# A Mamba layer stack on one core: scaled identities for the scan's inputs, wide activations, and a planned order for every engine

## The reference

```python
h1 = relu(bn(einsum('bchw,oc->bohw', x, nin_w)))
xs = concatenate([v, flip(v, 2), flip(v, 1), flip(v, (1, 2))])     # four directions
u, z = split(einsum('blc,ic->bli', xs, in_proj_w))                  # 256 channels each
uc = silu(causal_conv4(u) + conv_b)
dtr, B, C = split(uc @ x_proj_w.T)                                  # 8, 16, 16 columns
dt = softplus(dtr @ dt_proj_w.T + dt_proj_b)
h_t = exp(dt_t * A) * h_{t-1} + (dt_t * u_t) * B_t                  # 16 states per channel
y_t = sum_n h_t[n] * C_t[n]
out = ((y + uc * D) * silu(z)) @ out_proj_w.T
```

## Time and profile before

| | us |
|---|---|
| Median of three runs | 13713.5 |
| The profiled execution, its own time | 13695.55 |
| Its span, first to last instruction | 13693.8 |
| POOL busy | 13045.4 (95%) |
| DVE busy | 12477.9 (91%) |
| ACT busy | 11898.3 (87%) |
| PE busy | 11889.6 (87%) |
| Mean granted clock of TensorE | 0.946 of full speed |

### The profile page before, as it was taken

The page is one execution under the profiler, slowest core; times in us unless marked ns, Lnnn a source line. Parts: engine busy times, 40 slices in busy tenths (PEclk is TensorE's granted clock), DMA queues, the critical chain, the costliest instruction groups (busy, mean ns, idle before and its releaser), DMA issues.

```text
span 13693.8 us, 182039 instructions
## 1 busy us (share of the span) xinstructions
PE 11889.6 (87%) x67228; PEld 8271.3 (60%) x67228; DVE 12477.9 (91%) x8406; ACT 11898.3 (87%) x18047; POOL 13045.4 (95%) x3978
## 2 busy tenths in 40 slices
PE   7888888888888888888888888888888888888886
PEld 4566666666666666566666566665666666666654
DVE  7899999999999999999999999999999999999985
ACT  6888888888888888888888888888888888888884
POOL 7999999999999999999999999999999999999995
PEclk8999999999999999999999999999999999999997
DMA  5566566656566666566665665655666656666552
GB/s 191 224 226 228 228 224 230 235 224 229 221 235 232 228 228 226 226 230 233 226 230 221 233 231 226 230 226 226 234 230 225 230 223 230 233 227 228 226 213 115
DMA packets 544698, 3067.83 MB, mean 224 GB/s; under 512 B 60378, under 2 KB 60474, under 8 KB 281538
## 3 DMA queue, kind: packets, MB, share of 16 engines
q1 hardware_dynamic: 543810, 3056.18, 59.1%
HBM read 2990.40 MB, written 48.76 MB: 222 GB/s over the span
## 4 chain that ended last, share of the span: by engine, by line
POOL 33%; PE 22%; issue 16%; ACT 13%; DVE 9%; DMA 4%; POOLq 0%; DVEq 0%; SPq 0%; ACTq 0%
POOL ring L983 24%; PE work L1481 10%; POOL ring L966 8%; PE y_acc L1496 7%; DVE ring L1469 6%; ACT ring L1160 3%; ACT L1000 3%; DMA cb_rows_scratch<-stack 2%; PE y_acc L1481 2%; DVE slot L1455 2%; PE slot L1496 1%; DMA b_rows<-cb_rows_scratch 1%; PE slot L1481 1%; ACT slot L1160 1%; ACT z_t L1069 1%
## 5 line engine op out<-in xcount | busy, mean ns | idle before, releaser
L983 POOL TENSOR_TENSOR ring<-ring,c_rows 128x2048 f32<-128x2048 f32 x2048 | 9297.0, 4548 | 392.6 <-DVE ring L1469 375.4
L1469 DVE TENSOR_TENSOR_SCAN ring<-ring,slot 128x1024 f32<-128x1024 f32 x2560 | 5817.8, 2280 | 218.7 <-PE slot L1496 82.3
L1496 PE MATMUL y_acc<-wk,ring 128*128 128x128 f32 x32768 | 4513.7, 284 | 671.7 <-POOL ring L983 656.5
L1496 PEld LDWEIGHTS y_acc<-wk,ring 128*128 128x128 f32 x32768 | 3984.0, 147 | 1506.1 <-POOL ring L983 850.8
L1469 DVE TENSOR_TENSOR_SCAN ring<-slot,ring 128x1024 f32<-128x1024 f32 x1536 | 3495.0, 2276 | 370.4 <-POOL ring L966 266.4
L966 POOL TENSOR_TENSOR ring<-du,b_rows 128x1024 f32<-128x1024 f32 x1536 | 3634.2, 2369 | 64.7 <-DMA b_rows<-cb_rows_scratch 53.3
L1160 ACT ACTIVATE ring<-dt,a_neg 128x1024 f32<-128x1024 f32 x2560 | 2846.2, 1139 | 19.6 <-PE y_acc L1496 9.8
L1000 ACT ACT_TABLE_LOAD x1883 | 2415.9, 1283 | 33.7
L1455 DVE TENSOR_TENSOR slot<-du,slot 128x1024 f32<-128x1024 f32 x1856 | 2246.1, 1210 | 73.5 <-PE slot L1481 71.4
L1481 PE MATMUL work<-h_new,fused 128*128 128x512 f32 x4096 | 1936.5, 603 | 8.6 <-DVE padded L1334 3.1
L1160 ACT ACTIVATE slot<-dt,a_neg 128x1024 f32<-128x1024 f32 x1536 | 1707.1, 1113 | 240.6 <-DVE ring L1469 230.6
(11 more groups left out here) (178 smaller groups left out, 9934.9 us busy)
## 6 DMA issues: line engine op xcount, KB each, us to landing
c_rows<-cb_rows_scratch SPq DMA_DIRECT2D x2048, 1024.0 KB, 4.7
b_rows<-cb_rows_scratch SPq DMA_DIRECT2D x1536, 512.0 KB, 5.6
x_next<-in_x SPq DMA_DIRECT2D x32, 512.0 KB, 5.6
x_new_scratch<-x_next SPq DMA_DIRECT2D x32, 512.0 KB, 7.8
h_old<-h_new SPq DMA_DIRECT2D x32, 512.0 KB, 7.9
x_old<-x_new_scratch SPq DMA_DIRECT2D x32, 512.0 KB, 10.1
out<-x_old SPq DMA_DIRECT2D x32, 512.0 KB, 7.9
cb_rows_scratch<-stack SPq DMA_DIRECT2D x128, 116.0 KB
```

Of the source, the lines that this page charges most:

```text
L983: pool.tensor_tensor(pair, pair, c_rows[:, k % CB_BUFS, :, :], ALU.mult).then_inc(prod_ready, 1)
L1469: dve.tensor_tensor_scan(slot, a, b, 0.0, MUL, ADD).then_inc(scan_done, 1)
L1496: ins = pe.matmul(chunk(out_t, j), chunk(x, j), kc("ident"), is_transpose=True, start=start and j % (BANK // P) == 0, stop=stop, skip_grou ...
```

## The change

- **Kinds.** 46 D, 46 P and 36 Z units.
- **Z units.** ACT now scales the 128x128 identity, not du_t, by the B of the tokens (`zmul`, kc("ident") in place of du_t). The tile depends on direction and state alone, so both channel halves use it: 18 tiles per image serve 36 units. Six tiles are kept (`Z_BUFS`). PE multiplies du_t by the tile, an ordinary FP32 matmul (`turn_z`), where it was a transpose.
- **Wide steps.** silu, softplus, dt_copy and dt_u take both PSUM banks in one instruction of 1024 columns.
- **Passes.** The order of halves within directions alternates, so that the second pass of a direction and the first of the next have the same half and add up in `y_acc`: takes go from 7 to 5, and half of the adds of `yz` into `y_acc` fall away.
- **Group norm sums** of layers 1 to 3 come from the copies that write x (`accum_out`) in place of separate passes.
- **Free order.** Units' inputs and products, spreads and sums, b and scan are streams of their own in the planner, with new costs and shifts; an input may come as early as its ring slot is free. The planner does not look at the row loads, apart from those after a new direction's rows.
- **Buffers.** `CB_BUFS`, `B_BUFS` 4 to 3, three u_conv tiles for four. `store_rows` moves from SP to ACT, right behind the step that fills the rows.
- Decays of P units are in PSUM as before.

```diff
-KINDS = ('DPDPZDDDDPZPDPDZ', 'DPDZDPDZDPZPDPDP', 'DDDDDPZPDPPPZDDP', 'DPDPDPZZPPZZDPDP',
+KINDS = ('DDPPZPZPPDZDZZPP', 'DPPDZDZPPDZDZZPP', 'DDPDZPZDDPZDPPZZ', 'DDDDZPZPDPZPPPZZ',
 ...
-CB_BUFS = 4
-B_BUFS = 4
-Z_BUFS = 2
+CB_BUFS = 3
+B_BUFS = 3
+Z_BUFS = 6
+Z_STEPS = 4
 ...
-SUM_LATER = 4
 SHIFTS = [
-    (-413, 123, -1143, -1629, -1503, -1060, -1344, -1469, -1469, -2434, -2294, -1545, -1418, -1624, -1701, -489,
+    (-41, -1, 17, -17, 247, 112, -42, 84, -281, 71, 39, 41, -29, 121, -143, -315, -355, -257, -182, -36, -141, -301,
 ...
+def unit_flows(kind):
+    of = lambda *kinds: [u for u in range(UNITS) if kind_of(u) in kinds]
+    turned = of("D", "Z")[kind != "first":] + [UNITS] * (kind != "last")
+    return {"D": [[("b", u) for u in of("D")], [("scan", u) for u in range(UNITS)]],
+            "G": [[("input", u) for u in of("P")], [("prod", u) for u in range(1, UNITS, 2)]],
+            "P": [[("zturn" if kind_of(u) == "Z" else "spread", u) for u in turned], [("sum", u) for u in range(UNITS)]],
+            "A": [[("decay", u) for u in range(UNITS)]]}
 ...
-            def store_rows(d, base, rows_done):
-                sp.wait_ge(*done(base, rows_done))
-                sp.dma_start(cb_dram[d].rearrange("(n t) -> n t", t=TOK), cb_rows).then_inc(cb_out, 16)
+            def store_rows(d, rows_done):
+                act.wait_ge(*rows_done)
+                act.dma_start(cb_dram[d].rearrange("(n t) -> n t", t=TOK), cb_rows).then_inc(cb_out, 16)
 ...
-                if k >= CB_BUFS or s > 0:
-                    sp.wait_ge(prod_ready, s * PAIRS + k - CB_BUFS + 1)
+                if loads >= CB_BUFS:
+                    sp.wait_ge(prod_ready, loads - CB_BUFS + 1)
 ...
-                    for j in range(4 * i, 4 * i + 4):
-                        ins = act.activation(z_t[:, turned % Z_BUFS, j * P:(j + 1) * P], du_t[:, j * P:(j + 1) * P], ACT.Copy,
-                                             scale=b_t[:, d % 2, j * NST + n:j * NST + n + 1])
+                    for j in range(CH // Z_STEPS * i, CH // Z_STEPS * (i + 1)):
+                        ins = act.activation(z_t[:, tile_of(u), j * P:(j + 1) * P], kc("ident"), ACT.Copy,
+                                             scale=b_turned(d, s)[:, j * NST + n:j * NST + n + 1])
 ...
-                    ins = act.activation(w, w, ACT.Softplus, bias=kc("dt_b", name[2], name[2] + 1))
+                    ins = act.activation(both_banks(w), both_banks(w), ACT.Softplus, bias=kc("dt_b", name[2], name[2] + 1))
 ...
-                    turn(operand[u % 2], z_t[:, (s * N_Z + number("Z", u)) % Z_BUFS, :], True, True).then_inc(z_turned, 1)
+                    for j in range(CH):
+                        ins = mm(chunk(operand[u % 2], j), chunk(du_t, j), chunk(z_t[:, tile_of(u), :], j),
+                                 j % (BANK // P) == 0, True)
+                    ins.then_inc(z_turned, 1)
```

More of the change, by code:

```diff
@@ L143, in silu_pair, with conv, gate_z, project @@
             steps += [step((name, d, h, *k, c), "P", key(c), after if not steps else [])]
-    return steps + [step(("silu", of, d, h, c), "A", key(c)) for c in range(2)]
-def operands(d, first=False):
-    steps = []
[L150 to L155, removed]
+    return steps + [step(("silu", of, d, h), "A", both(key(0), key(1)))]
+def conv(d, h):
+    return silu_pair("u", d, h, "conv_in", [(k,) for k in range(TAPS)])
+def gate_z(f, h, after=()):
+    return silu_pair("z", f, h, "z", [()], after)
+def project(d):
+    steps = []
     for c in range(2):
@@ L515, in lay @@
         t, i, e = best
-        change = TABLE_LOAD * (table_of(e, i) != table)
-        table = table_of(e, i)
-        if i < 0:
-            op, place = programs[e][at[e]]
-            at[e] += 1
-            end[op] = free[e] = t + unit_cost(op) + change
+        change = TABLE_LOAD * (table_of(i) != table)
+        table = table_of(i)
+        name, _, bank, after = lines[i][heads[i]]
+        if i < sides:
+            free[e] = t + unit_cost(name) + change
+            end[name] = free[e] + LATENCY[e]
+            plan.append((name, e, 0, None))
+            heads[i] += 1
             continue
-        name, _, bank, after = streams[i][heads[i]]
-        place = programs[e][at[e]][1] if at[e] < len(programs[e]) else END[e]
-        waits = list(after) + ([streams[i][heads[i] - 1][0]] if heads[i] else ["start"])
-        if bank is not None and bank not in held[i]:
+        waits = list(after) + ([lines[i][heads[i] - 1][0]] if heads[i] else ["start"])
+        if any(b not in held[i] for b in banks_of(bank)):
             w = banks.index(min(banks))
@@ L602, in image_streams @@
     takes = []
-    for p in range(PASSES - 1):
-        f, t, h = p // 4, p // 2 % 2, p % 2
-        after = [("sum", p * NST + NST - 1)]
-        if t == 0 and not first:
+    for p in TAKES:
+        f, h = p // 4, parts_of(p)[1]
+        after = [("sum", p * NST + NST - 1)] + ([("silu", "z", f, h)] if p % 4 else [])
+        if not first and p % 4 != 3:
             after += [(("post", 1) if h else ("angles",)) if f else ("mix", 4, 1)]
-        takes += [step(("take", p), "D" if t else "A", None, after)]
-        if t:
+        takes += [step(("take", p), "D" if p % 4 else "A", None, after)]
+        if p % 4:
             takes += turn_y("this", f, h)
@@ L1691, in image @@
-                side_steps(END["P"])
+                    turn(y_acc, ring[:, u % RING, :], starts, ends).then_inc(sum_done, 1)
+                for name, _, bank, after in order_of(plans[kind], "P"):
+                    if name[0] == "spread":
+                        spread_b(name[1])
+                    elif name[0] == "zturn":
+                        turn_z(name[1])
+                    elif name[0] == "sum":
+                        add_y(name[1])
+                    else:
+                        hold(pe, "P", base, of, after)
+                        step(name, image_of(name, s), bank_of[bank])
```

585 lines of the change are left out of this document (316 added, 269 removed), and 98 rows, old and new, of the table SHIFTS.

## The result

The changed kernel takes 14764.2 us (median of 4 runs, 14761.5 to 14780.8) against 13713.6 us: 1.077 times the time before, 95% interval 1.0752 to 1.0790. The forecast was slower, for late rows of B, at 13950 us, in a range of 13610 to 14390. The direction came out, and the late rows are there; the time is 814 us above the forecast and 374 us above the range.

The account below looks back on a forecast made before the run. POOL bounds the kernel: a middle image takes 402.6 + 23.3 + 2 = 427.9 us against 419.1, 8.8 more, x 30 = 264; 13695.6 + 264 - 9 = 13950 us, range 13610 to 14390.

Parts of the forecast that it names:

- POOL's work: POOL's busy time per image: 48 inputs become 46 at 2.37 us each, so 407.3 becomes 402.6 us.
- DVE 372.6 and ACT 328: Busy time per image of the two engines: DVE falls from 388.2 to 372.6 us, ACT from 369.8 to about 328.
- PE: PE's busy time per image: 36 plain products replace 22 turns, 367.4 becomes 402.8 us, staying under POOL.
- The factor of four: Skill's FP32 transpose advantage: a plain product would take 3.5 us, PE 61 us more per image; given no chance.
- Late rows: POOL's inputs wait for b_rows loads queued behind a pair's c_rows load: 23.3 us per middle image; chance 0.70.
- the walk: Stepwise calculation of POOL's order in a middle image, rows landing in 5.5 us: 13.1 us at units 66 to 76, 10.2 elsewhere.
- Waits for scans: POOL's waits for scans should mostly go: 2 us per image taken, bounds 0 and today's 11.8.
- Rival C: PE becomes the bound; if all its gaps stay, an image takes 454 us and the time is 14750 us; chance 0.06.
- My argument against C: Back to back, PE needs a fifth less than its busy time, so it should not become the bound.
- Rival A: Row loads are in time: 402.6 + 3 to 10 us per image, near 13400 us; chance 0.18 in both forms.
- Three buffers alone: Three c_rows buffers cost nothing: two products, 9.1 us, lie between issue and use, and c_rows lands in 4.5.
- The sign that I had given for a wrong size: The forecast would be wrong in size if the b_rows landings were far from 5.5 us.

Follow-up runs that it names:

- e1: Changed kernel with SP issuing row loads in the order in which POOL frees their buffers, not pair by pair: 13964.1 us, ratio 1.0193.
- e3: Changed kernel with row loads in order of release and transposes in place of the Z units' plain products (multiplication by du_t left out): 13740.6 us, ratio 1.0030.
- e9: e1 with a second searched order of the middle images' steps, walked with dearer spreads and a slower TensorE after longer waits: 13557.4 us, ratio 0.9897.
- e5: Kernel before, with Z tiles put through eight plain products with the identity in place of eight turns: 13898.0 us, ratio 1.0139.
- e4: Kernel before, with three c_rows and three b_rows buffers for four (small setup scratch areas moved): 13792.7 us, ratio 1.0067.
- e8: e1 with a first searched order of the middle images' steps, found by moving single steps and walking the result: 13804.4 us, ratio 1.0068.
- e6: Changed kernel, pairwise loads kept, with POOL's inputs held back behind the product of two pairs before their own: 14648.3 us, ratio 1.0684.

## Why the prediction was wrong in size

Step by step, per image, prediction against trace:

- **POOL's work**, 402.6: 403.0. DVE 372.6 and ACT 328: 374.9 and 333.8 by the window's sums / 32. Right, or 2% low.
- **PE**, 402.8: 405.6. Right, with the Z unit's product at 2.07 us and not 1.98. The factor of four that the Trainium skill states ("TensorE: Matmul & The Clock Gate", "Terms") would have made a Z unit 3.5 us, an estimate from that factor and the 0.88 us of the turns; the trace has 2.07, so the row decided rightly.
- **Late rows**, 23.3: 27.2 as waits, 25.3 as time (e1). The mechanism holds at the place and in the numbers shown above, where the late rows landed in 5.5 to 6.2 us and the waits are 14.0 us against 13.1. The difference lies at the other places of that image, 13.7 us for the 10.2 of the walk: three of their rows landed in 6.8 to 7.3 us, not 5.5.
- **Waits for scans**, "I take 2", with bounds of 0 and 11.8: 20.0. **This is the step that failed**: 18.0 of the 26.6 us by which the image is longer than the 427.9 forecast. The late rows are 3.9 more; the rest is mostly in small waits of POOL for other steps, 2.6 us per image between 3000 and 9000 us, which the sum left out. I took the old waits for the ceiling, since DVE and ACT get lighter and inputs come earlier. But a wait of a new order is not bounded by the waits of the old one. e3 and e9 show its parts: of the 9.1 us per image by which e1 is above before, 7.4 are the product; the rest, together with the 4.3 us of work that POOL saved and did not get, I put down to the order itself: e9's order takes 13.5 us per image out of e1's with the same work but for a table load.
- **Rival C** said that if all of PE's gaps stay, the image is 454 us and the time 14750. Image and time came out so (454.5, 14764), but e1 refutes the story: 25 of the 34 us were loads, and e9 runs with PE at 94% of the span. That a rival's number is hit does not make it the cause; here it is chance. My argument against C was too strong as well: back to back the turns take a fifth less than by their busy time, but the plain products only a tenth (1.78 against 1.98). What C had right is that PE, serving in order, passes part of its work on: 24% of the product's estimated time in the changed kernel, 33% in the old order (e5), 8% in e9's.
- **Rival A** ("loads in time": 402.6 + 3 to 10, near 13400) is wrong on the loads, which were late, and on the rest too: with loads in time the kernel takes 13964. With the order mended too it takes 13557.
- **Three buffers alone**, "hidden": 3.3 us per image in the old order (e4), for a row of B behind the store and not for c_rows. The order without that store in the queue does not pay it.

So 34.4 us more per image = 25.3 late rows + 7.4 product + 1.7 for the rest, the last being 4.3 of saved work against about 6 of new waits. The forecast had 23.3, 0 (hidden) and -14.5 (4.7 less work and 9.8 of scan waits that should go). The product's 7.4 belongs to the same failed step: I saw PE at 402.8 of 428 us, called it under POOL, and priced it at nothing. The sign that I had given for a wrong size, landings far from 5.5 us, did not show this: at the walked place they were not far.

What stays open: whether the clock or the mispriced spread held back e8 more, and what the free order would lose with four buffers and the pairwise queue.

## What to carry to other kernels

When an order is freed, free the queue that feeds it in the same edit: a load queue in order of use is a queue in order of use only for the old order. When a change moves work onto an engine that serves in order and is nearly as busy as the busiest, do not price it at nothing: here, with TensorE at 87 to 94% of the span, 8 to 33% of it was visible, and the order decided how much. When the profile names a releaser that had long been done, look up when the row landed: in e4 the waits "for DVE" were waits for a load. And never bound the waits of a new order by those of the old one: walk the other engines too, with durations from the trace for every step that something stands behind, the small ones as well.

## What the runs showed of the hardware

- A row's load (512 KB) lands in 6.1 us in the median when it is issued together with a pair's 1 MB, in 4.3 us when each is issued as its buffer comes free (e1; 3.2 at least). Before, with four buffers, it was 5.6. These medians are of different orders too (e6, pairwise, has 5.6), so the issue beside the 1 MB is not shown to be the only reason.
- A load that waits for a store in the same queue holds all that stands behind it: SyncE's queue stood 9.3 us in e4 at 7169 us, and 899 us in 95 such stops over the run.
- Slow stretches of TensorE's clock follow short waits in these traces: after 1.95 us of waiting, 14 us at a granted clock of 0.63 (e8, above). In the changed kernel the stretch 7052 to 7070, with waits of 0.67 and 1.15 us, has 0.81. Over the run the clock is 0.946 before and 0.942 after, 0.961 in e1, 0.962 in e8, and 0.971 in e9, whose order was chosen with that in mind.
- Eight plain FP32 products of 128x128 take about twice as long as eight turns: 2.07 us by the group (after) against 1.11 (before), 1.78 against 0.88 back to back. Replaced one by one, they were worth 6.2 us per image in the old order (22 units), 7.4 in the changed order and 2.4 in e9's (36 units each): the same operation, three prices.
